# Expert routing spread over projections and batches, pair sums on VectorE, the third layer's bias tables loaded under the sums, and late step sizes on GpSimd

## The chip, the cores and the metric

One core of one Trainium2 chip runs the whole program in one launch. The metric is the device time of that launch in microseconds; lower is better. Five queues of instructions run side by side and meet at semaphores: TensorE (PE), VectorE (DVE), ScalarE (ACT), GpSimd (POOL) and SyncE (SP), which here only issues DMAs.

## What is computed

Four layers on x, 8 sequences of 256 tokens of 128 channels (2048 tokens). Each layer is

```
xn = layernorm(x);  s = mixer(xn);  g = silu(ffn(xn));  x = x + s * g
```

- First layer: a gated linear recurrence, and a dense product of FP8-valued weights.
- Second layer: attention of 16 heads of 8 channels, with binarized weights, and a mixture of 8 experts of which each token takes two. For each choice the reference takes a softmax over the scores that lie within 2 x 0.01 (relative) of the chosen one: `mult = exp(t - s) / sum`, with masked scores left out.
- Third layer: attention of 16 heads with a relative position bias: `scores += 8 * rel_bias[bucket(k - q)]`, 32 buckets, and a gated FFN of 384 units.
- Fourth layer: a selective scan (`h = exp(dt*A)*h + dt*u*B`, `y = sum_n C*h`) with 256 channels and 16 states, and 8 experts of hidden size 512 with a capacity of 256 rows each.

## The kernel before

Everything stays in SBUF with channels on the partitions and the 2048 tokens along the row, in four chunks of 512. Each engine's queue is written out by hand, layer by layer.

**Norm** (`norm_pe`, L222 and L226; `norm_act`, L245 to L257; `norm_dve`, L240): centre by a matmul, square, mean by a matmul, `exp(-0.5 * ln)`, multiply. It follows the chunks of the residual (`residual_dve`, L2103 and L2105).

**Attention** (second and third layer, `attn_pe`, `attn_act`, `attn_dve`, `attn_pool`). First the projections, chunk by chunk: PE projects q and k (L610), ACT writes the upper half in float16 (`high`, L760), DVE the rest (`low`, L841), PE spreads both to strips of 32 rows (L648, L649; six PSUM banks in turn), ACT keeps q (L776) and DVE keeps k (L869). Then the eight sequences ("batches") go through one list of steps that all engines walk, `STEPS[l]`, made from `ORDER`: S1.0 to S1.7 are scores for the row maxima of the next batch (PE L712, DVE L917 or, with the bias, L930), NM negates the maxima (L911), MT puts them beside q (PE L680, L685, ACT L791), S2.0 to S2.7 are the scores again (PE L723, and L731 for the bias) with the exponential by ACT (L804), PV multiplies by v (PE L743), and O, D, R, Y finish the previous batch. Before the first batch all eight S1 steps run alone. S1, S2, MT and two more steps take three pairs of PSUM banks in turn.

**Routing of the second layer** rides on that list through `EXTRA`. TC (`route1_choose`, 13 DVE instructions on 128x128) picks both experts, after S1.7 of the lead-in. TN (`route1_near`, 9 more) makes the masks, in batch 0, followed by CT (counts by PE) and EX (two exponentials by ACT). In batch 1 GpSimd makes the softmax sums (`route1_sums`) and the rows' destinations (`route1_place`, some 50 small instructions in a chain), and from batch 2 it issues 32 indirect DMAs (`route1_dispatch`). XT transposes the tokens. One eighth of the expert weights per batch is split into two float16 halves: ACT writes the upper (WH, L823), GpSimd the lower (`low_weights`, L1262 to L1265, after the routing in each batch), ACT puts the upper back (WB, L826, behind O of the next batch). So WB waits for GpSimd.

**Expert tiles** (`moe_pe`, `moe_act`, `moe_dve`, `moe_pool`): 39 tiles, GpSimd scatters each result to DRAM; `moe_sums` (SP, L1414) reads back the two results of each token, and PE adds each pair by two float32 matmuls with the identity (L1334, 32 products).

**Bias tables of the third layer**: after the second layer's residual the one-hot table is loaded, PE makes the bias rows (L602), ACT scales them (L754), SP writes them to DRAM (L2148) and reads them back as three tables: `bias_q` (3 MB, L2150, into `wf`, which held expert weights) and two halves of `band32` (L2153, into `gate` and `s_sb`). After the projections DVE makes eight small instructions from `bias_q` (L877 to L884), ACT the upper half of `band32` in float16 (L785), GpSimd the lower (L970).

**Scan loop** (`l3_pe`, `l3_act`, `l3_dve`, `l3_pool`, `l3_sync`): 64 tiles of 128x1024. For tile i ACT makes `exp(dt*A)` in PSUM (L1829), GpSimd `dt*u*B` (L2029, four buffers), DVE scans (L1948) and multiplies by C (L1955), PE sums y (L1692); experts ride along at fixed tiles. DVE makes the step sizes of the third and fourth quarter (`step_sizes`, L1925, L1926) after tiles 10 and 12. GpSimd sums the two dispatched halves (L2039) at tiles 14 and 15, PE transposes the sums (L1627) and ACT keeps them (L1800).

## Time and profile before

| | |
|---|---|
| median of 3 runs | 991.57 us (990.63 to 996.0) |
| the profiled execution | 993.26 us, its span 991.5 us |
| PE, DVE busy | 784.5 us (79%), 703.8 us (71%) |
| ACT, POOL busy | 480.4 us, 368.9 us |
| mean granted clock of TensorE | 0.892 |
| chain that ended last | PE 45%, DVE 21%, issue 15%, ACT 11%, POOL 5% |

The stages, in us from the span's start: first layer to 115; second layer's projections 115 to 149, batches to 304, expert tiles to 373, sums, residual and norm to 401; third layer's projections to 433, batches to 612, FFN to 640; fourth layer's preparation to 719, loop to 977, end to 991. No engine is full over the whole, so the shares above say little of one edit; each has to be read from its stage.

### The profile page before, as it was taken

The numbers are of one execution on the slowest core, as the hardware profiler recorded it, in microseconds if no ns is written. First come the engines' busy times: TensorE is split into PE (matmuls) and PEld (weight loads), VectorE is DVE, ScalarE is ACT, GpSimd is POOL, SyncE is SP. The second block draws the span as 40 slices with busy tenths as digits, with TensorE's granted clock in tenths as the row PEclk, the third lists the DMA queues.
The fourth block names the chain that finished last, engine by engine and source line by source line (L and its number), as shares of the span: only waits on it lengthen the run. The fifth ranks groups of instructions, "written<-read, shape, count | busy, mean of one in ns | idle before, by whom it ended". The sixth has DMA issues, their size and how long they took to land.

```text
span 991.5 us, 13685 instructions
## 1 busy us (share of the span) xinstructions
PE 784.5 (79%) x4872; PEld 400.4 (40%) x4872; DVE 703.8 (71%) x1361; ACT 480.4 (48%) x699; POOL 368.9 (37%) x368
## 2 busy tenths in 40 slices
PE   5883795867988996857999998987464678788787
PEld 2331451323435765423555554453121344444344
DVE  2989478656755662586777751268589889889997
ACT  4465352645784443442555563255533245454463
POOL 0000201447662552020000000001797868888860
PEclk9997795777898997885999998978779889999999
DMA  9300000000024113510000000022346525445351
GB/s 364 162 1 0 4 0 1 2 6 29 29 69 134 38 34 91 182 43 1 2 1 2 2 3 1 0 85 69 101 158 189 169 70 205 147 170 177 132 173 43
DMA packets 44339, 76.56 MB, mean 77 GB/s; under 512 B 8479, under 2 KB 30472, under 8 KB 43248
## 3 DMA queue, kind: packets, MB, share of 16 engines
q1 hardware_dynamic: 39952, 67.96, 20.9%
q0 software_dynamic: 4320, 7.72, 2.3%
q8 instruction: 40, 0.66, 0.3%
q14 instruction: 27, 0.22, 0.1%
HBM read 59.83 MB, written 17.01 MB: 78 GB/s over the span
## 4 chain that ended last, share of the span: by engine, by line
PE 45%; DVE 21%; issue 15%; ACT 11%; POOL 5%; DMA 1%; DVEq 0%; SPq 0%; POOLq 0%; ACTq 0%
DVE band L1955 5%; PE ps L743 5%; PE ps L731 4%; DVE arena L1948 4%; PE ps L723 3%; PE ps L290 3%; PE ps L712 2%; ACT arena L804 2%; DVE ttr_out L930 2%; ACT ps L1829 2%; PE ps L610 2%; POOL exp_in L1988 2%; PE ps L704 2%; PE ps L1299 1%; PE ps L649 1%
## 5 line engine op out<-in xcount | busy, mean ns | idle before, releaser
L1948 DVE TENSOR_TENSOR_SCAN arena<-ps,arena 128x1024 f32<-128x1024 f32 x64 | 146.6, 2290 | 27.9 <-ACT ps L1829 13.9
L804 ACT ACTIVATE arena<-ps 128x1024 f32<-128x1024 f32 x128 | 128.3, 1025 | 71.3 <-PE ps L731 54.2
L1829 ACT ACTIVATE ps<-arena,negA 128x1024 f32<-128x1024 f32 x64 | 71.6, 1118 | 131.5 <-DVE arena L1948 131.5
L1692 PE MATMUL ps<-band,w 128*128 128x512 f32 x256 | 123.3, 606 | 0.0
L930 DVE CUSTOM_DVE_ANT_0 ttr_out<-ps,wf 128x256 bf16<-128x256 f32 x256 | 93.1, 420 | 28.3 <-issue 18.0
L1614 PE MATMUL ps<-xq,sel 128*128 128x512 bf16 x128 | 41.2, 405 | 76.7 <-DVE band L1955 67.9
L917 DVE TENSOR_REDUCE arena<-ps 128x4 f32<-128x1024 f32 x64 | 77.1, 1223 | 34.1 <-PE ps L712 33.0
L2029 POOL TENSOR_TENSOR arena<-arena 128x1024 f32<-128x1024 f32 x32 | 76.3, 2387 | 12.5 <-DVE arena L1948 12.1
L712 PE MATMUL ps<-arena 32*128 32x256 f16 x512 | 53.5, 304 | 34.6 <-ACT arena L804 13.3
L1955 DVE TENSOR_TENSOR band<-arena,ps 128x1024 f32<-128x1024 f32 x64 | 76.6, 1197 | 3.5 <-PE ps L1614 3.5
L2029 POOL TENSOR_TENSOR arena<-arena,gate 128x1024 f32<-128x1024 f32 x32 | 75.0, 2361 | 9.9 <-DVE arena L1948 7.7
L1988 POOL DMA_INDIRECT exp_in<-wf,wa x32 | 31.4, 983 | 124.9 <-ACT wf L1729 116.7
L743 PE MATMUL ps<-arena 128*32 128x256 f32 x1024 | 76.2, 420 | 1.0 <-ACT arena L804 0.9
L978 POOL COPY arena<-arena 128x128 f32<-128x128 f32 x32 | 8.5, 296 | 179.5 <-PE ps L743 149.5
L723 PE MATMUL ps<-arena 32*128 32x256 f16 x512 | 62.6, 295 | 9.8 <-DVE arena L917 4.5
L1692 PEld LDWEIGHTS ps<-band,w 128*128 128x128 f32 x256 | 50.4, 197 | 44.6 <-issue 35.7
L731 PE MATMUL ps<-band,ident 128*128 128x192 f16 (+1 forms) x512 | 60.0, 242 | 0.0
L1400 POOL DMA_INDIRECT e_out<-arena,band x39 | 37.9, 972 | 42.8 <-ACT arena L1358 30.6
L1614 PEld LDWEIGHTS ps<-xq,sel 128*128 128x128 bf16 x128 | 8.1, 99 | 108.1 <-DVE band L1955 97.0
L943 POOL MEMSET arena<- 128x512 f16 x2 | 1.0, 524 | 121.6 <-DVE xT L2105 121.6
L791 ACT ACTIVATE arena<-ps 128x1024 f16<-128x1024 f32 x16 | 16.4, 1024 | 54.9 <-PE ps L685 54.9
L712 PEld LDWEIGHTS ps<-arena 32*128 32x128 f16 x512 | 14.7, 95 | 66.0 <-ACT arena L804 19.1
(366 smaller groups left out, 1622.3 us busy)
## 6 DMA issues: line engine op xcount, KB each, us to landing
gate<-b_dram SPq DMA_DIRECT2D x32, 512.0 KB, 4.6
arena<-b_dram SPq DMA_DIRECT2D x32, 512.0 KB, 4.1
wf<-pack1f_dram SPq DMA_DIRECT2D x1, 3076.0 KB, 15.2
wf<-bias_rows SPq DMA_DIRECT2D x1, 3072.0 KB, 10.4
exp_in<-band SPq DMA_DIRECT2D x2, 1032.0 KB, 18.9
exp_out<-band SPq DMA_DIRECT2D x2, 1024.0 KB, 20.8
e_in<-band SPq DMA_DIRECT2D x2, 1024.0 KB, 25.5
arena<-e_out SPq DMA_DIRECT2D x8, 256.0 KB, 4.8
```

The source lines that it names most:

```text
L712: mm = pe.matmul(out_[:, a:a + SEQ], q_st[h, g, (b + 1) * SEQ + qb * P:(b + 1) * SEQ + (qb + 1) * P], k_st[h, g, (b + 1) * SEQ:(b + 2) * S ...
L723: mm = pe.matmul(out_[:, a:a + SEQ], k_st[h, g, b * SEQ + kb * P:b * SEQ + (kb + 1) * P], q_b[par][h, g, :], start=True, stop=(l == 1))
L731: mm = pe.matmul(out_[:, a:a + n], ident16[:, :], band16[:, part, g * HH + 2 * pr + j, 0:n], start=False, stop=(part == 1))
L743: mm = pe.matmul(ps[32 * h:32 * h + 32, 6, (i // 2) * SEQ:(i // 2 + 1) * SEQ], v_b[pp][:, kb, i * HH + h, :], probs[i % 2][:, h, kb, :], s ...
L804: act.activation(probs[g % 2][:, 2 * pr:2 * pr + 2, :, :].rearrange("p h k n -> p (h k n)"), PAIRS[l][("S2", i, b)], ACT.Exp).then_inc(A[" ...
L917: dve.tensor_reduce(row_max[1 - par][:, :, g, 2 * pr:2 * pr + 2].rearrange("p b h -> p h b"), PAIRS[l][("S1", i, b)].rearrange("p (h b n) ...
L930: ins = dve.tensor_tensor_reduce(ttr_out[:, n, :], PAIRS[l][("S1", i, b)][:, n * SEQ:(n + 1) * SEQ], bias_q[:, g * HH + h, WIN - a - SEQ:W ...
L1692: mm = pe.matmul(ps[:, j, :], ident, hc[i % 2][:, j * CH:(j + 1) * CH], start=False, stop=True, skip_group_check=True)
L1829: act.activation(dA_ps, dt3[:, cb, hf * HALF:(hf + 1) * HALF], ACT.Exp, scale=negA[:, cb * STATE + n:cb * STATE + n + 1]).then_inc(M["dA"], 1)
L1948: dve.tensor_tensor_scan(hst[i % 2], dA_ps, dbu[i % 4], 0.0, ALU.mult, ALU.add).then_inc(M["scan"], 1)
L1955: dve.tensor_tensor(hc[i % 2], hst[i % 2], pair(3), ALU.mult).then_inc(M["hc"], 1)
L2029: pool.tensor_tensor(dbu[i % 4], du[:, cb, hf * HALF:(hf + 1) * HALF], b_sb[i % 4], ALU.mult).then_inc(M["dbu"], 1)
```

## The change

**Routing.** The choice is cut into its two rounds (`top1`), which DVE makes behind chunks 0 and 1 of the projections, and the masks behind chunk 2. Both exponentials come before the list of steps, CT in the lead-in before NM, XT one batch earlier, RC at S1.4 of batch 1 and TE at S1.4 of batch 2. On GpSimd the sums run in the lead-in, the totals (`route1_totals`, the first half of the placing) in batch 0, the rest in batch 1; in each batch `low_weights` now comes first. WB stands at S2.4 of the same batch, WH of the next eighth at S2.6.

**Pair sums.** DVE adds the pairs (four instructions of 128x512), PE transposes the sum (16 instructions).

**Bias tables.** The one-hot load, the two products, the scaling and the write to DRAM stand before the sums; the reads stand behind the loads of the sums, the key rows behind them. One half of `band32` goes to `x_rows`, the other still waits for the residual. DVE's eight instructions stand before the projections, ACT's two in them, GpSimd's two during them.

**Step sizes.** Third and fourth quarter on GpSimd: a sum behind tiles 12 and 16, a product behind 14 and 18. DVE's index instructions go from four to two.

The core of the diff:

```diff
-        EXTRA = {(-1, "S1", 7): [("TC", 0)], (0, "S2", 3): [("TN", 0)], (0, "S2", 4): [("CT", 0)], (0, "S2", 5): [("EX", 0), ("EX", 1)],
-                 (2, "S1", 2): [("RC", 0)], (2, "S1", 6): [("TE", 0)],
-                 (1, "S2", 5): [("XT", 0)], (2, "S2", 5): [("XT", 1)]}
+        EXTRA = {(-1, "S1", 7): [("CT", 0)], (0, "S2", 5): [("XT", 0)], (1, "S1", 4): [("RC", 0)], (1, "S2", 5): [("XT", 1)],
+                 (2, "S1", 4): [("TE", 0)]}
...
-                        if (kind, i) == ("O", 0) and b >= 1:
-                            steps.append(("WB", b - 1, b))
-                        if (kind, i) == ("S2", 2) and 0 <= b < BATCH:
-                            steps.append(("WH", b, b))
+                        if (kind, i) == ("S2", 4) and 0 <= b < BATCH:
+                            steps.append(("WB", b, b))
+                        if (kind, i) == ("S2", 6) and 0 <= b < BATCH - 1:
+                            steps.append(("WH", b + 1, b))
...
@@ attn_act @@
+            if l == 2:
+                act.wait_ge(tabs_in, 32)
+                act.wait_ge(S3["zeroed"], 16 * 7)
+                for i, t in enumerate(band32):
+                    act.activation(band16[:, 0, i * HEADS // 2:(i + 1) * HEADS // 2, :], t[:, :, ::-1], ACT.Copy).then_inc(rows_ready, 1)
             high(2)
             high(3)
...
+            if l == 1:
+                route1_exps(act)
+                act.wait_ge(rest_in, 64)
+                act.activation(w_hi, w_part(0), ACT.Copy, scale=W_UP).then_inc(MOE["w_hi"], 1)
...
@@ attn_dve @@
+            step(dve.memset(neg_max, 0.0))
+            if l == 2:
+                dve.wait_ge(rows_out, 32)
+                step(dve.tensor_copy(b_far[:, 0, :], bias_q[:, :, 0]))
...
+                if l == 1:
+                    if c < 2:
+                        route1_choose(dve, c + 1)
+                    elif c == 2:
+                        route1_near(dve)
...
@@ attn_pool @@
                 if l == 1:
+                    if 0 <= b < BATCH:
+                        low_weights(pool, b)
                     if b == -1:
                         route1_both(pool)
+                        route1_sums(pool)
+                    elif b == 0:
+                        route1_totals(pool)
                     elif b == 1:
-                        route1_sums(pool)
                         route1_place(pool)
-                    elif 2 <= b < BATCH:
+                    elif b < BATCH:
                         route1_dispatch(pool, b - 2)
-                    if 0 <= b < BATCH:
-                        low_weights(pool, b)
...
@@ moe_pe @@
+            pe.wait_ge(wa2_in, 16)
+            pe.wait_ge(oh_in, 16)
+            for j in range(2):
+                mm = pe.matmul(ps[0:HEADS, 4 + j, :], WA(1, "rel_bias")[0:BUCKETS, :], onehot_sb[:, j * DIST:(j + 1) * DIST],
+                               start=True, stop=True)
+            mm.then_inc(rows_ps, 1)
             for c in range(NCH):
-                pe.wait_ge(*MOE.at("y_in%d" % c, 32))
+                pe.wait_ge(*MOE.at("y_sum", c + 1))
                 for t in range(4):
-                    for k in range(2):
-                        mm = pe.matmul(ps[:, c, t * P:(t + 1) * P], y1[k][:, 4 * c + t, :], ident, start=(k == 0), stop=(k == 1))
+                    mm = pe.transpose(ps[:, c, t * P:(t + 1) * P], y1[0][:, 4 * c + t, :], ident)
...
@@ moe_dve @@
+            for c in range(NCH):
+                dve.wait_ge(*MOE.at("y_in%d" % c, 32))
+                a_, b_ = (y1[k][:, 4 * c:4 * c + 4, :] for k in range(2))
+                dve.tensor_tensor(a_, a_, b_, ALU.add).then_inc(MOE["y_sum"], 1)
...
@@ l3_dve, l3_pool @@
-                if i in (10, 12):
-                    step_sizes(i // 2 - 3)
...
+                if i in (12, 16):
+                    q = i // 4 - 1
+                    pool.wait_ge(M["plus"], 4 * (q // NB) + 4)
+                    pool.wait_ge(M["ln"], q + 1)
+                    pool.tensor_tensor(quarter(dt3, q), quarter(dt3, q), quarter(sp3, q), ALU.add).then_inc(M["pool_step"], 1)
+                elif i in (14, 18):
+                    q = i // 4 - 1
+                    pool.wait_ge(M["pool_step"], q - 1)
+                    pool.tensor_tensor(quarter(du, q), quarter(dt3, q), quarter(uc, q), ALU.mult).then_inc(M["du"], 1)
```

GpSimd's queue in the second layer, batch 1, before: L978 copies v, L1198 begins the sums, L1211 the placing (its rows up to L1241 are left out), L1262 to L1265 split the weights.

```order
L1265 COPY wf<-w 128x2x256
L978 COPY arena<-arena 128x4x4x8 x2
L1198 TENSOR_TENSOR band<-band 128x128
L1199 COPY band<-band 128x128
...
L1241 TENSOR_SCALAR band<-band 128x8
L1262 TENSOR_SCALAR wf<-wf 128x512
L1263 TENSOR_TENSOR w<-wf,w 128x512
L1265 COPY wf<-w 128x2x256
```

The same place now: L1260 to L1263 split the weights, L1225 begins what is left of the placing.

```order
L966 COPY arena<-arena 128x4x4x8 x2
L1260 TENSOR_SCALAR wf<-wf 128x512
L1261 TENSOR_TENSOR w<-wf,w 128x512
L1263 COPY wf<-w 128x2x256
L1225 TENSOR_TENSOR band<-band 128x8
L1226 TENSOR_SCALAR band<-band 128x8
...
L1239 TENSOR_SCALAR band<-band 128x8
```

The split of the weights moved from behind the chain to right behind the copy of v.

VectorE in the second layer's projections now (L869 keeps k, L843 is `low`, L1037 to L1043 the first round of the choice):

```order
L869 TENSOR_TENSOR arena<-ps,arena 128x512 x4
L843 SCALAR_TENSOR_TENSOR arena<-ps,bq_s,arena 128x512
L843 SCALAR_TENSOR_TENSOR arena<-ps,wa,arena 128x512
L1037 TENSOR_REDUCE band<-band 128x16
L1038 TENSOR_TENSOR band<-band 128x128
L1039 TENSOR_TENSOR band<-band,wc 128x128
L1040 TENSOR_REDUCE band<-band 128x16
L1041 TENSOR_TENSOR band<-band 128x128
L1043 SCALAR_TENSOR_TENSOR band<-band 128x128
L869 TENSOR_TENSOR arena<-ps,arena 128x512 x4
```

Before, the next L869 followed the two `low` at once, and the choice stood behind the eight L917.

SyncE between the expert tiles and the fourth layer's weights, before (`e_out` rows are the sums, `far_keys` the key rows):

```order
L1414 DMA arena<-e_out 128x4x128 x8
L2144 DMA arena<-onehot_dram 32x1024
L2130 DMA arena<-far_keys_dram 5x512 x4
L2148 DMA bias_rows<-arena 16x2x512
L2150 DMA wf<-bias_rows 128x16x384
L2153 DMA gate<-bias_rows 128x8x192
L2153 DMA s_sb<-bias_rows 128x8x192
```

And now:

```order
L2162 DMA bias_rows<-arena 16x2x512
L1423 DMA arena<-e_out 128x4x128 x8
L2165 DMA wf<-bias_rows 128x16x384
L2170 DMA arena<-bias_rows 128x8x192
L2170 DMA s_sb<-bias_rows 128x8x192
L2148 DMA arena<-far_keys_dram 5x512 x4
```

The write of the bias rows moved ahead of the eight loads of the sums, the one-hot load to the start of the expert tiles, and the key rows to the end.

## Rows read from the trace of the kernel before

**Rows 1.** PE in order of time: each batch's L685, and two waits.

```profile
162.82 1.03 PE L685 MATMUL ps<-ident,arena 128*128 128x128 f16 x8 [4.21 <-DVE arena L911]
182.70 1.06 PE L685 MATMUL ps<-ident,arena 128*128 128x128 f16 x8
197.94 0.61 PE L685 MATMUL ps<-ident,arena 128*128 128x128 f16 x8
209.17 0.60 PE L712 MATMUL ps<-arena 32*128 32x256 f16 x4 [7.26 <-ACT arena L804]
222.29 0.62 PE L685 MATMUL ps<-ident,arena 128*128 128x128 f16 x8
231.69 0.60 PE L712 MATMUL ps<-arena 32*128 32x256 f16 x4 [5.42 <-ACT arena L804]
242.91 0.61 PE L685 MATMUL ps<-ident,arena 128*128 128x128 f16 x8
```

**Rows 2.** Batches 4 and 6: stretch, busy PE, PEld, DVE, ACT, POOL, clock, DMA share, GB/s.

```profile
242.90:257.35 14.45, 13.31 (x162) 6.02 (x161) 12.01 (x14) 10.66 (x13) 8.76 (x10) 0.88 0.07 24
271.96:284.80 12.84, 11.68 (x158) 5.38 (x156) 11.71 (x13) 10.66 (x13) 9.41 (x12) 1.00 0.08 27
```

**Rows 3.** ACT's L826 behind GpSimd's split of the weights, batch 2.

```profile
207.58 0.63 ACT L826 ACTIVATE wf<-w 128x512 f16<-128x512 f16 x1 [7.04 <-POOL w L1263]
```

**Rows 4.** DVE in order of time, projections and choice: start, us, what.

```profile
137.41 1.89 DVE L869 TENSOR_TENSOR arena<-ps,arena 128x512 f16<-128x512 f32 x3
148.73 0.06 DVE L873 MEMSET wait_here<- 1x1 f32 x1
158.56 0.28 DVE L1050 TENSOR_REDUCE band<-band 128x16 f32<-128x128 f32 x1
162.33 0.28 DVE L1154 TENSOR_TENSOR band<-band 128x128 f32<-128x128 f32 x1
```

**Rows 5.** The sums: SP, PE, a stretch, last residual, bias rows' products.

```profile
376.17 5.36 SPq L1414 DMA_DIRECT2D arena<-e_out  x8
379.96 10.06 PE L1334 MATMUL ps<-w,arena 128*128 128x128 f32 x64 [7.10 <-DMA arena<-e_out]
380.00:384.00 4.00, 4.00 (x19) 4.00 (x20) 0.00 (x0) 0.22 (x1) 0.00 (x0) 0.50 1.08 298
391.41 0.69 DVE L2105 TENSOR_TENSOR xT<-xT,gate 128x512 f32<-128x512 f32 x1
401.59 2.59 PE L602 MATMUL ps<-arena,wa 32*16 32x512 f32 x4 [3.08 <-DVE xn L240]
```

**Rows 6.** Bias tables: landing of L2150, then ACT, DVE, POOL, PE.

```profile
DMA to landing us min/median/max: 10.4/10.4/10.4
432.45 1.48 ACT L785 ACTIVATE band<-gate 128x1536 f16<-128x1536 f32 x1
434.15 3.01 DVE L884 CAST arena<-b_far 128x16 f16<-128x16 f32 x1
434.00 3.10 POOL L970 TENSOR_TENSOR band<-gate,band 128x1536 f16<-128x1536 f32 x1 [20.42 <-ACT band L785]
441.87 0.61 PE L712 MATMUL ps<-arena 32*128 32x256 f16 x4 [7.90 <-DVE arena L930]
```

**Rows 7.** The loop: DVE's step sizes and a wait, POOL's wait.

```profile
758.70 5.03 DVE L1925 TENSOR_TENSOR arena<-arena 128x1024 f32<-128x1024 f32 x1
765.12 2.29 DVE L1948 TENSOR_TENSOR_SCAN arena<-ps,arena 128x1024 f32<-128x1024 f32 x1
771.98 1.22 DVE L1925 TENSOR_TENSOR arena<-arena 128x1024 f32<-128x1024 f32 x1
775.54 2.29 DVE L1948 TENSOR_TENSOR_SCAN arena<-ps,arena 128x1024 f32<-128x1024 f32 x1
770.79 3.53 POOL L2039 TENSOR_TENSOR wf<-wf,s_sb 128x512 f32<-128x512 f32 x2 [8.16 <-DMA wa<-exp_in]
760.30 2.33 POOL L2029 TENSOR_TENSOR arena<-arena 128x1024 f32<-128x1024 f32 x1
```

More of the change, by code:

```diff
@@ L501, in build @@
         bias_q = wf[:, 0:HEADS * WIN].rearrange("p (h n) -> p h n", h=HEADS)
-        band32 = [t.rearrange("p (h n) -> p h n", n=BAND) for t in (gate[:, 0:HEADS * BAND // 2], s_sb[:, TOK - HEADS * BAND // 2:])]
+        band32 = [t.rearrange("p (h n) -> p h n", n=BAND) for t in (x_rows.rearrange("p t d -> p (t d)")[:, 0:HEADS * BAND // 2], s_sb[:, TOK - HEADS * BAND // 2:])]
         onehot_sb = probs[0].rearrange("p h k n -> p (h k n)")[0:BUCKETS, 0:2 * DIST]
@@ L751, in attn_act @@
             act.wait_ge(*A.at("bq_done", 1))
-            if l == 2:
-                act.wait_ge(rows_ps, 1)
-                act.activation(rows_sb, pair(2)[0:HEADS, :], ACT.Copy, scale=8.0).then_inc(rows_ready, 1)
             def high(n):
@@ L960, in attn_pool @@
             assert made[0] == ALL_ZEROED
+            if l == 2:
+                for i, t in enumerate(band32):
+                    pool.wait_ge(rows_ready, 2 + i)
+                    heads = slice(i * HEADS // 2, (i + 1) * HEADS // 2)
+                    pool.tensor_tensor(band16[:, 1, heads, :], t[:, :, ::-1], band16[:, 0, heads, :], ALU.subtract)\
+                        .then_inc(A["v_zeroed"], 1)
             pool.wait_ge(*A.at("v_done", 4))
@@ L1213, in route1_place @@
                 run = to
+            assert run is runs1[1]
             step(pool.tensor_scalar(tiles1, run[:, NT - 1, :], 1.0 / P, 0.5 - 0.5 / P, ALU.mult, ALU.add))
@@ L1226, in route1_place @@
                 step(ins) if d < 32 else ins.then_inc(MOE["m_in"], 1)
-            step(pool.tensor_tensor(first1, end, tiles1, ALU.subtract))
+        def route1_place(pool):
+            step = route1_step(pool)
+            run, total, before_ = runs1[1], counts_of(1), counts_of(0)
+            step(pool.tensor_tensor(first1, ends_of(3), tiles1, ALU.subtract))
             step(pool.tensor_scalar(first1, first1, float(P), None, ALU.mult))
@@ L1358, in moe_act @@
                     act.activation(e1_sb[n % 4], ps[:, 7, 0:P], ACT.Copy).then_inc(MOE["eo"], 1)
+            act.wait_ge(rows_ps, 1)
+            act.activation(rows_sb, pair(2)[0:HEADS, :], ACT.Copy, scale=8.0).then_inc(rows_ready, 1)
             for c in range(NCH):
```

130 lines of the change are left out of this document (51 added, 79 removed).

## The prediction

> **What bounds the kernel now.** I read the page first, for the two busy shares (PE 79%, DVE 71%) and the chain's 15% "issue", which say that no engine is full and that the time lies in hand-overs. Then the chain of waits in order of time, to find where the chain leaves its usual pattern, and then each engine's timeline at those places. Four places stand out, and the change touches all four.
>
> The second layer's eight batches. PE's L685 marks each batch [rows 1]. Batch 0 takes 182.70 - 162.82 = 19.9 us, batch 1 15.2, batch 2 24.4, batch 3 20.6, and batches 4 and 6 14.45 and 12.84 [rows 2]. In batches 2 and 3 PE sits idle 7.26 and 5.42 us for ACT's exponential [rows 1]. ACT itself is not busy then: its L826 had waited 7.04 us for GpSimd's L1263 [rows 3], which stood in GpSimd's queue behind the chain of small routing instructions (batch 2) and behind six scatters (batch 3). Ahead of batch 0 PE waits 4.21 us for L911 [rows 1]; the choice of experts, 158.56 to 162.61, is what DVE does in that gap [rows 4].
>
> The sums. SP issues the loads at 376.17, PE starts at 379.96 and is busy 10.06 us with 64 half products [rows 5], first at the granted clock of 0.50, which is 1.2 GHz.
>
> The third layer's start. PE spends 2.59 us on the bias rows between norm and projections [rows 5], and after the projections stands still 7.90 us before the second S1 step [rows 6]: DVE is making the small table instructions, of which L884 took 3.01 us for 16 columns, exactly while GpSimd's L970 (3.10 us) ran.
>
> The loop. DVE is its bound: a scan of 2.29 and a product by C follow each other. The step sizes interrupt it from 758.70 to 765.12 and from 771.98 to 775.54 [rows 7].
>
> **The change part by part.** All durations are of the profiled execution, 993.26 us with a span of 991.5; the median is 991.57, so I take the sum of the differences off 991.57.
>
> *Projections of the second layer.* DVE gets 22 instructions on 128x128 (6, then 7, then 9). Thirteen of them took 162.61 - 158.56 = 4.05 us, 0.31 each with their step waits [rows 4], so 22 cost 6.9 us. What room has DVE? From 137.41 to 148.73 it makes twelve L869 of 0.63 (7.6 us) and two `low`, for which I allow 1.5: some 2.3 us are free. PE can run six banks ahead, which shifts this room but adds none. So the projections end 6.9 - 2.3 = 4.6 us later; the bounds are 2 (more room) and 9 (all 6.9, and PE, waiting more, falls to 1.2 GHz).
>
> *Lead-in.* The choice goes: -4.05 us. What is late next is MT's first product, which now follows CT in the ring of three pairs and waits for the last reduction; it was done early. I take +0.8, one L685 or less (0.61 to 1.03).
>
> *Batch 0* loses CT and the nine mask instructions on DVE, whose product delayed S1; it gains one transposition with its 1.02 us eviction by ACT. The stretch ran at 1.2 GHz before and starts so again. I take -2.6, between +1 and -6 (a free batch). Batch 1 swaps one XT for the other: 0.
>
> *Batches 2 and 3.* GpSimd's split comes first in each batch, so L826's wait goes. GpSimd then has per batch 0.5 for v, 3.3 for the split and at most 6 scatters of 1.3: under 12 us, inside a batch. The split is ready some 5.5 us into the batch, S2.4 comes at about 8. Both batches come to a free one, between 12.84 and 14.45 [rows 2]; I take 13.7: -10.7 and -6.9. Batches 4 and 5 may lose the dip of the clock (0.88 against 1.00 in batch 6), since WB and WH no longer stand ahead of the early exponentials: -0.7 and -0.9, and -0.5 at the tail. For PE leaving the upper level more often than I think I give back 1. Sum for the second layer: 4.6 - 4.05 + 0.8 - 2.6 - 10.7 - 6.9 - 1.6 - 0.5 + 1 = -20.0, bounds -10 and -27. Behind it the last scatters end some 4 us later relative to the batches; before, the first load of expert rows landed 5 us ahead of its use, so this costs nothing, or up to 2 if that room is smaller.
>
> *Sums.* The bias products (2.59), ACT's scaling and one DMA issue now stand before the loads: these start at 377.1 instead of 376.17, +0.9. The data is in by about 385.5 (at 298 GB/s the DMAs were done at 384.6 [rows 5]). DVE adds the last pair by 386.2, PE transposes in 0.6, ACT's last gate is at 387.5 against 390.7, but DVE makes its four residual pairs (1.4 us each) only after its four sums, so the last is at 391.9 against 392.1 [rows 5]. The norm starts 1.8 earlier on ACT and is paced by PE: -1.2, between -3 and +3.
>
> Before, PE had come back to 2.4 GHz inside the 64 products. The 16 transposes are a quarter of the records, and the norm's products could run at 1.2 GHz, 1.7 us instead of 0.9 for a pair; that is the +3. The Trainium skill (TensorE: Matmul & The Clock Gate, "PE-mode transpose") says that transposes don't count as busy for the clock in the way products do. No row here shows a transpose alone raising or not raising the clock; by the page the term would be about +2 instead of -1.2.
>
> *Bias rows out of the norm's shadow:* -2.59 for L602, of which I give back 0.4 for a colder start of the projections: -2.2.
>
> *Tables.* `bias_q` is queued right behind the sums' loads; with its 10.4 us to landing [rows 6] it is there at about 396, the second `band32`, behind the residual, at about 403. DVE asks at 400, ACT at 411: hidden, with 4 us to spare; beyond that each us late is lost. ACT's two L785 (2 x 1.48) now stand between the eviction of the output weights and `high` of chunk 1, with PE, and DVE's `low`, behind them. Six banks cover part: +1.6, between 0 and 3. The lead-in then starts without the tables: of the 7.90 us, S1's usual 1.03 and its first step remain: -6.3 (-5.5 to -7).
>
> GpSimd's two L970 now run beside DVE's L869. Before, L884, which reads and writes SBUF alone, was held up by L970. The L869 and `low` have one operand in PSUM, as the scan and L1955 have, which kept 2.29 and 1.20 us beside GpSimd's L2029. So I charge nothing.
>
> *Loop.* Two interruptions go: 6.42 + 3.56 = -10.0. GpSimd gets four instructions of 2.33 each [rows 7] and two small ones. The first two fall into its wait of 8.16 us [rows 7], covered. The last two, behind tiles 16 and 18, aren't: GpSimd, three tiles ahead before, is about level at tiles 16 to 19, which I price at 1.5; two index instructions less on DVE give 0.5: -9.0, between -4 and -10.5.
>
> Sum: -20.0 - 1.2 - 2.2 + 1.6 - 6.3 - 9.0 = -37.1. **991.57 - 37.1 = 954.5 us.**
>
> **The rivals.**
>
> *A, the forecast:* 954.5, own range 948 to 961. Chance 0.60.
>
> *B, the batches keep half.* PE drops to 1.2 GHz in the busier projections and in batch 0 and the batches settle at 14.5 or above with WB waiting now and then: the second layer gives 10, not 20: 964.5. For it: batches 4 and 5 stood at 0.88 without any GpSimd wait. Against it: batch 6 ran at 1.00 with the same work [rows 2]. Chance 0.18.
>
> *C, GpSimd's products cost DVE what they save.* L1925 took 5.03 us with GpSimd's L2029 beside it and 1.22 without [rows 7]: two engines, one in the other's way. If scans were held by the four new instructions, 4 x 2.33 = 9.3 come back: 963.8. Against it: scans ran at 2.29 beside L2029 throughout. The Trainium skill (Perfetto Trace Analysis, "Optimizing Scalar/DVE Operations") warns that work moved between these two might not help because they share an SBUF port. Chance 0.12.
>
> *D, the tables are late.* If the 3 MB land at 405 or later, DVE's first `low` and all behind it wait, 8 us: 962.5. For it: the same queue carries the sums' 2 MB first. Against it: 298 GB/s on those. Chance 0.05.
>
> *E, slower: low clock through the batches.* If the more even mix kept PE at 1.2 GHz from the projections on, a batch's 13.3 us of PE at 0.88 [rows 2] become 23.4; over seven batches +68 against my 13.7, hence 1022. It makes the kernel slower only once the mean batch is over 13.7 + 37/7 = 19 us, as batch 0 was. Against it: batches 1 and 6. Chance 0.02; another 0.03 is for a sum of small losses that leaves no change.
>
> **How the numbers follow.** A, B, C and D (0.95) are all faster by over 0.5% (below 986.6), which is also about what a measurement of this kernel tells from no change; 0.03 within, 0.02 slower. The range takes A with its bounds, and B, C and D up to a little above their centres: 946 to 967.
>
> **What would show it.** In the profile after: the choice's instructions between the L869, and the first S1 step 4 to 5 us later; no wait of ACT's L826 for GpSimd over 1 us; eight batches of 12.8 to 14.5 us but the first two; the four DVE additions at about 381 to 386, and the norm ending 1 us earlier; no pause over 2 us before the second S1 step of the third layer; scans every 3.5 us from tile 0 to 14, and the scan of tile 15 about 9 us earlier relative to tile 0. I am wrong if the second layer's batches still hold a GpSimd wait, if DVE's first `low` in the third layer waits for a DMA, or if scans wait for L2029 in many tiles.

## The result and the profile after

The changed kernel takes 968.27 us (median of 4 runs, 967.06 to 969.62) against 992.83 us of the kernel before in the same runs (990.63 to 996.0): ratio 0.9751, 95% interval 0.9719 to 0.9783. It is faster, as forecast, but by 24.6 us and not 37. 968.3 is nearer to rival B's time (964.5) than to the forecast's, and lies 1.3 us above the range. Of the 13.8 us between forecast and result, 1.3 is the kernel before itself: the forecast took its 37.1 off a median of 991.57, which is 992.83 with a fourth run. The profiled span is 967.5 us against 991.5.

The working is checked most easily by milestones that both traces have. Each row is the length of a piece (us, before and after), and what the prediction said of it.

| Piece | before | after | measured | predicted |
|---|---|---|---|---|
| second layer's projections (scaling of bq to first S1 maximum) | 34.47 | 37.49 | +3.0 | +4.6 |
| lead-in to the first MT | 13.32 | 10.02 | -3.3 | -3.25 |
| batch 0 | 19.88 | 17.15 | -2.7 | -2.6 |
| batch 1 | 15.24 | 16.82 | +1.6 | 0 |
| batches 2 and 3 | 44.97 | 31.27 | -13.7 | -17.6 |
| batches 4, 5 and 6 | 41.70 | 46.09 | +4.4 | -1.6 |
| batch 7 and tail | 18.96 | 19.67 | +0.7 | -0.5 (+1 given back) |
| experts, sums and norm, to its end | 98.02 | 98.28 | +0.3 | -1.2 |
| bias rows' products | 2.52 | 0 | -2.5 | -2.2 |
| third layer's projections | 29.25 | 30.67 | +1.4 | +1.6 |
| its lead-in (S1) | 20.27 | 13.72 | -6.5 | -6.3 |
| its first batch | 21.86 | 24.07 | +2.2 | 0 |
| loop, first scan to last | 253.76 | 244.70 | -9.1 | -9.0 |

The changed trace comes to this point 0.6 us later, and the pieces not listed differ by -0.4 together; the sum is -24.0.

The second layer is where the time is missing: 20 us were promised and 10.0 came (the first seven rows). Its batches by stretches (length, busy time of PE, PEld, DVE, ACT and POOL, granted clock, DMA share, GB/s), to be read beside [rows 2]:

```profile
180.27:197.09 16.82, 13.67 (x168) 6.80 (x167) 13.14 (x15) 11.50 (x14) 9.78 (x25) 0.90 0.00 1
197.09:213.08 15.99, 13.05 (x159) 5.89 (x158) 13.89 (x17) 10.62 (x13) 10.64 (x13) 0.89 0.07 22
213.08:228.36 15.28, 12.96 (x159) 5.85 (x158) 12.85 (x14) 10.66 (x13) 8.70 (x10) 0.89 0.09 29
228.36:244.57 16.21, 13.94 (x160) 6.20 (x159) 12.94 (x14) 10.59 (x13) 8.70 (x10) 0.79 0.07 22
244.57:260.36 15.79, 12.90 (x159) 5.76 (x158) 13.03 (x14) 10.59 (x13) 10.21 (x13) 0.89 0.08 27
260.36:274.45 14.09, 11.39 (x155) 5.16 (x154) 12.74 (x13) 10.59 (x13) 10.29 (x12) 1.00 0.08 25
```

No batch is at the 13.7 us of the forecast, though no instruction stands at a semaphore for GpSimd: the waits of [rows 1] and [rows 3] are gone. What TensorE waits for between 163 and 294 us says more (what waits, for whom: us in all, times, longest):

```profile
PE ps L690 <- DVE arena L892: 10.0, 8, 1.7
PE ps L715 <- DVE arena L905: 5.1, 9, 1.1
PE ps L715 <- ACT arena L798: 3.6, 8, 0.5
```

L892 ends VectorE's chain of three instructions (reciprocal of the denominators, its upper half as f16, the rest). VectorE in batch 4 of the changed kernel, and GpSimd at that time:

```profile
231.80 0.95 DVE L888 RECIPROCAL arena<-ps 128x128 f32<-128x128 f32 x1
232.78 0.92 DVE L890 CAST arena<-arena 128x128 f16<-128x128 f32 x1
233.73 0.70 DVE L892 TENSOR_TENSOR arena<-arena 128x128 f16<-128x128 f32 x1
```

```profile
230.88 1.49 POOL L1260 TENSOR_SCALAR wf<-wf 128x512 f32<-128x512 f32 x1
232.46 1.16 POOL L1261 TENSOR_TENSOR w<-wf,w 128x512 f16<-128x512 f32 x1
233.68 0.61 POOL L1263 COPY wf<-w 128x512 f16<-128x512 f16 x1
```

The two instructions that read and write SBUF take 0.92 and 0.70. In batch 6 of the kernel before, where GpSimd issued scatters at that time, they took 0.23 and 0.29:

```profile
276.22 0.23 DVE L902 CAST arena<-arena 128x128 f16<-128x128 f32 x1
276.48 0.29 DVE L904 TENSOR_TENSOR arena<-arena 128x128 f16<-128x128 f32 x1
```

The reciprocal reads PSUM and takes 0.95 in both. TensorE starts R late and runs the PV product behind it at 1.2 GHz, 1.94 us, where others take 1.07.

```profile
234.49 0.29 PE L690 MATMUL ps<-arena,spread 128*128 128x128 f16 x1 [1.23 <-DVE arena L892]
236.00 1.94 PE L735 MATMUL ps<-arena 128*32 128x256 f32 x16
```

The loop came out at the number forecast, but not by its working. The first row below is the scan of tile 15, the second that of tile 16, the third one of VectorE's two index instructions, the last GpSimd's work on the expert rows:

```profile
761.33 2.29 DVE L1959 TENSOR_TENSOR_SCAN arena<-ps,arena 128x1024 f32<-128x1024 f32 x1 [3.34 <-POOL arena L2036]
766.09 2.29 DVE L1959 TENSOR_TENSOR_SCAN arena<-ps,arena 128x1024 f32<-128x1024 f32 x1 [1.36 <-POOL arena L2036]
770.70 2.28 DVE L1983 SCALAR_TENSOR_TENSOR wa<-wa 128x32 uint32<-128x32 f32 x1
756.45 2.49 POOL L2057 TENSOR_TENSOR wf<-wf,s_sb 128x512 f32<-128x512 f32 x2 [3.82 <-DMA wa<-exp_in]
```

Scans now wait for GpSimd, which in turn waits for rows of the experts from DRAM, as in [rows 7]. The index instruction of 32 columns takes 2.28 beside a product of GpSimd's; in step_sizes_on_dve, below, the same one takes 0.19.

### The profile page after: what moved, and what is told of

The parts are those of the page before. It is cut to its first block, busy times and chain, and to the rows that moved or that the text cites. A ratio compares the mean times of both kernels' runs of the same rounds, so it can differ in the third digit from the quotient of the medians.

```text
span 967.5 us, 13578 instructions
## 1 busy us (share of the span) xinstructions
PE 774.8 (80%) x4811; PEld 393.7 (41%) x4824; DVE 695.5 (72%) x1357; ACT 479.2 (50%) x699; POOL 375.8 (39%) x374
## 4 chain that ended last, share of the span: by engine, by line
PE 47%; DVE 21%; issue 13%; ACT 11%; POOL 4%; DMA 2%; SPq 2%; DVEq 0%; POOLq 0%
PE ps L735 6%; PE ps L723 5%; DVE band L1966 4%; DVE arena L1959 3%; PE ps L715 3%; PE ps L704 3%; PE ps L290 3%; POOL arena L2036 2%; POOL exp_in L1995 2%; DVE ttr_out L918 2%; PE ps L696 2%; DVE arena L905 2%; ACT ps L1838 2%; PE ps L1314 2%; PE ps L1297 2%
## 5 line engine op out<-in xcount | busy, mean ns | idle before, releaser
L918 DVE CUSTOM_DVE_ANT_0 ttr_out<-ps,wf 128x256 bf16<-128x256 f32 x256 | 93.1, 420 | 30.7 <-issue 21.7
L1623 PE MATMUL ps<-xq,sel 128*128 128x512 bf16 x116 | 37.5, 398 | 71.9 <-DVE band L1966 62.6
L704 PE MATMUL ps<-arena 32*128 32x256 f16 x512 | 54.2, 305 | 13.7 <-DVE arena L918 6.6
L723 PEld LDWEIGHTS ps<-band,ident 128*128 128x128 f16 x512 | 33.9, 100 | 19.3 <-issue 8.3
L715 PEld LDWEIGHTS ps<-arena 32*128 32x128 f16 x512 | 21.4, 95 | 49.0 <-issue 17.7
## 6 DMA issues: line engine op xcount, KB each, us to landing
wf<-pack1f_dram SPq DMA_DIRECT2D x1, 3076.0 KB, 15.5
wf<-bias_rows SPq DMA_DIRECT2D x1, 3072.0 KB, 12.8
exp_out<-band SPq DMA_DIRECT2D x2, 1024.0 KB, 21.2
```

The source lines that it names most:

```text
L704: mm = pe.matmul(out_[:, a:a + SEQ], q_st[h, g, (b + 1) * SEQ + qb * P:(b + 1) * SEQ + (qb + 1) * P], k_st[h, g, (b + 1) * SEQ:(b + 2) * S ...
L715: mm = pe.matmul(out_[:, a:a + SEQ], k_st[h, g, b * SEQ + kb * P:b * SEQ + (kb + 1) * P], q_b[par][h, g, :], start=True, stop=(l == 1))
L723: mm = pe.matmul(out_[:, a:a + n], ident16[:, :], band16[:, part, g * HH + 2 * pr + j, 0:n], start=False, stop=(part == 1))
L918: ins = dve.tensor_tensor_reduce(ttr_out[:, n, :], PAIRS[l][("S1", i, b)][:, n * SEQ:(n + 1) * SEQ], bias_q[:, g * HH + h, WIN - a - SEQ:W ...
```

## The experiments

Theory P: GpSimd's split beside VectorE's chain holds the chain up, and this is why the batches stay at 16 us. Theory A: ScalarE's new order does it. Theory C: TensorE's clock does it by itself. For the loop: the interruptions were the 9 us, or something else was. Ratios are to the kernel before; the changed kernel has 0.9751 (0.9719 to 0.9783). Each time is a median of four executions, of which one was profiled; every stretch and wait comes from that one.

**split_waits**

```diff
+                    if 1 <= b < BATCH:
+                        pool.wait_ge(*A.at("d_done", b))
                     if 0 <= b < BATCH:
                         low_weights(pool, b)
```

> The changed kernel, but GpSimd's split of batches 1 to 7 waits until VectorE's three reciprocal instructions of that batch (D chain) are through. Theory P (GpSimd's split beside VectorE's chain): in the changed kernel the chain takes 0.95 + 0.92 + 0.70 = 2.6 us, without the split beside it 1.5 (as in batch 6 of the kernel before), and the PV step behind it runs at the upper clock more often (1.07 instead of 1.94); so 1.1 to 2 us off each of batches 1 to 6: the second layer's batches 7 to 12 us shorter, 956 to 961 us in all. Theory A (ScalarE's new order, with WB and WH among the exponentials, sets the batch's length): unchanged, 967 to 969. Theory C (the clock comes first, and falls whatever GpSimd does): chain shorter, but the batches shorter by under 3 us, 965 to 968.

958.58 us, ratio 0.9624 (0.9588 to 0.9659): 9.7 us less than the changed kernel, for one more wait. TensorE's waits for L892 fall from 10.0 to 2.6, and batches 2 to 6 from 77.4 to 69.8:

```profile
PE ps L690 <- DVE arena L892: 2.6, 3, 1.7
PE ps L1290 <- DMA gate<-e_in: 1.2, 1, 1.2
```

```profile
197.93:212.08 14.15, 12.74 (x159) 5.63 (x158) 13.18 (x17) 10.59 (x13) 7.62 (x10) 0.88 0.03 11
226.48:241.32 14.84, 12.90 (x159) 5.86 (x158) 12.21 (x14) 10.59 (x13) 9.13 (x11) 0.89 0.07 24
241.32:254.65 13.33, 11.72 (x160) 5.26 (x158) 11.75 (x14) 10.59 (x13) 7.08 (x10) 1.00 0.05 17
```

P holds and A falls, since ScalarE's order is the same. C explains the rest: a batch is at 13.1 to 13.3 with the clock at 1.00 and at 14.2 to 14.8 with 0.88. Not all of the 9.7 lies there. The experts start 5.2 us earlier (288.95 against 294.12), though 1.2 are lost to their first load, which is late now (the second row). The third layer is shorter by 2.7 up to its first MT and by 2.0 in its first batch, with no edit there: TensorE left 1.2 GHz earlier. Those 4.7 are no gain to count on, since both stretches differ by as much between other profiles of the same code (28.0 to 30.7 us for the projections, 21.0 to 24.1 for the first batch).

The batches themselves repeat. The seven other kernels whose split still runs beside the chain (choice_in_one_piece, the two sums runs and the first four of the loop, all below) have casts of 0.91 to 0.99 there and take 77.4 to 78.8 us for batches 2 to 6. The three in which it doesn't (split_waits, split_old_place, split_rows_steps) have casts of 0.23 to 0.29 and take 69.4 to 69.8.

**split_mixed**

```diff
+                    if b == 1:
+                        pool.wait_ge(*A.at("d_done", b))
+                    elif 2 <= b < BATCH:
+                        route1_dispatch(pool, b - 2, 0)
                     if 0 <= b < BATCH:
                         low_weights(pool, b)
```

Here `route1_dispatch` with 0 issues the first two scatters and with 1, at its old place, the others.

> The changed kernel, but GpSimd issues two of its scatters ahead of the split in batches 2 to 7, and waits for the chain only in batch 1. Theory P: as split_waits or up to 2 us better, since GpSimd doesn't stand idle and the next batch's copy of v isn't late: 955 to 961. Theory A: 967 to 969. Theory C: 965 to 968. If issuing indirect DMAs is what slows the chain (against P), the casts take over 0.4 us here.

966.14 us, 0.9688 (0.9635 to 0.9742), above P's range, and an interval that overlaps the changed kernel's. But it shows how finely this depends on time, as two scatters don't quite reach over the chain. In batch 5 the first scatter came late, behind two small instructions, and lay over the whole chain. In batch 6 the cast began 0.6 us before the end of the second scatter and was held until the split had begun:

```profile
247.58 0.23 DVE L890 CAST arena<-arena 128x128 f16<-128x128 f32 x1
263.42 0.67 DVE L890 CAST arena<-arena 128x128 f16<-128x128 f32 x1
264.12 0.70 DVE L892 TENSOR_TENSOR arena<-arena 128x128 f16<-128x128 f32 x1
```

```profile
263.04 0.98 POOL L1259 DMA_INDIRECT e_in<-arena,band  x1 [0.30 <-issue]
264.03 1.53 POOL L1265 TENSOR_SCALAR wf<-wf 128x512 f32<-128x512 f32 x1
```

Computing on SBUF costs the chain its 0.7 to 1 us. Issuing a scatter mostly costs it nothing: 0.23 in batches 4 to 7 of the kernel before and in batches 2 to 7 of split_old_place, each beside a scatter. It isn't always free, though. In batches 3, 4 and 6 here the cast began before the split did, and by its usual 0.23 it would have ended before it too; in batch 7 it took 0.45 in the changed kernel and 0.33 here beside scatters alone. As spans on GpSimd are rough, where the hold begins stays open. Batches 3, 4 and 6, with casts of 0.67, take 15.9, 15.5 and 15.35, and batch 2, with 0.23, 14.5. Batch 5 has 0.23 too and takes 15.8: there ScalarE's WB waits 0.82 us for the split, which now comes later. The clock differs too (0.79 in batch 3, 0.88 or 0.89 in the others), so that these lengths don't show the price of the cast by itself.

**split_old_place**

```diff
-                        if (kind, i) == ("S2", 4) and 0 <= b < BATCH:
-                            steps.append(("WB", b, b))
-                        if (kind, i) == ("S2", 6) and 0 <= b < BATCH - 1:
-                            steps.append(("WH", b + 1, b))
+                        if (kind, i) == ("O", 0) and b >= 1:
+                            steps.append(("WB", b - 1, b))
+                        if (kind, i) == ("S2", 2) and 1 <= b < BATCH:
+                            steps.append(("WH", b, b))
```

and `low_weights` behind the routing work on GpSimd.

> The changed kernel with the split where the kernel before had it: GpSimd behind the routing work and the scatters, ScalarE's copy back behind the next batch's O, its copy out behind S2.2; all else as changed. Theory P: batches 4 to 6 go back to 14.5, 14.6 and 12.8 (now 16.2, 15.8, 14.3: -4.4), batches 2 and 3 wait again for GpSimd, though less than before since sums and totals come earlier: batch 3 keeps its 5 us wait; net -4 to +3, 964 to 971. Theory A: the same direction, as ScalarE's order goes back too. It tells what the new place was worth by itself: the prediction said 19 us for batches 2 to 6; then this would be 985.

961.33 us, 0.9644 (0.9600 to 0.9687): better than the changed kernel by 7, outside what I expected. Its batches are 17.4, 17.2, 14.25, 14.6, 13.1, 14.6 and 12.8: the waits of [rows 1] don't come back. So the earlier routing work is enough to remove them, without the new place of the split; whether that place alone would have done it, no run shows. In batch 2 it was the chain of small instructions in front of the split. Batch 3 is another case: its six scatters still stand in front of the split here. Before, GpSimd had first stood still for 9.28 us until ScalarE had the transposed tokens, and this wait is gone with the earlier XT:

```profile
217.96 0.28 POOL L1253 TENSOR_SCALAR arena<-band 128x16 f32<-128x16 f32 x1 [9.28 <-ACT arena L816]
```

The casts are back at 0.23 to 0.28, with ScalarE's order and GpSimd's both as before; it is split_waits that tells the two apart. The new place of the split by itself costs about 7 us.

**choice_in_one_piece** puts the 22 choice instructions as one piece behind the projections.

> The changed kernel with the 22 instructions of the choice of experts not between the projections but in one piece behind them, ahead of the first S1 steps. Prediction (22 cost 6.9 us, 2.3 of them hidden beside the projections): first row maximum 2.3 us later than in the changed kernel: 155.4 instead of 153.1, and 970 in all. Rival H (beside the projections they are hidden nearly in full, since VectorE waits there for TensorE): 5 to 7 us later, 974. Rival N (nothing is hidden): the same time, 968.

970.51 us, 0.9777 (0.9747 to 0.9808). From the scaling of bq to the first S1 maximum it takes 41.48 us against 37.49 changed and 34.47 before. The piece takes 6.8 us (148.63 to 155.44), as priced, of which 4.0 are hidden among the projections where I had put 2.3. Of the whole, 2.2 us show, and the intervals overlap.

**sums_on_pe** and **sums_interleaved**

```diff
...
-                    mm = pe.transpose(ps[:, c, t * P:(t + 1) * P], y1[0][:, 4 * c + t, :], ident)
+                    for k in range(2):
+                        mm = pe.matmul(ps[:, c, t * P:(t + 1) * P], y1[k][:, 4 * c + t, :], ident, start=(k == 0), stop=(k == 1))
...
```

The first also takes VectorE's four additions out, and TensorE waits for the loads instead. The second leaves only the last chunk's residual behind the sums:

```diff
                 dve.tensor_tensor(a_, a_, b_, ALU.add).then_inc(MOE["y_sum"], 1)
+                if c:
+                    moe_residual(dve, (c - 1,))
```

> The changed kernel with the pair sums on TensorE again, by two products with the identity for each tile as in the kernel before; all else as changed. It prices the part by itself. The prediction: 1.2 us slower than the changed kernel. Rival T (16 transposes leave TensorE at 1.2 GHz and four norm products take 3.8 instead of 1.9 us, as the profile after shows, which eats the gain): 0 plus or minus 1.5 us, with the first four norm products at 1.9 us here. Rival, clock wins: 1 to 3 us faster.

> The changed kernel, but VectorE makes the residual of chunk c-1 right behind the pair sum of chunk c, instead of all four behind the four sums. Theory S (the norm starts late because VectorE does its residuals last): first norm product at 376.5 instead of 379.3, the norm over 1.5 to 2.5 us earlier, 966 in all. Rival (TensorE at 1.2 GHz and ScalarE's table load pace the norm): under 1 us, nothing measurable.

967.61 us, 0.9750 (0.9728 to 0.9771), and 969.71 us, 0.9778 (0.9749 to 0.9807): nothing that the intervals can tell, either way. The norm's first four products, in the changed kernel and in sums_on_pe:

```profile
379.26 3.78 PE L222 MATMUL ps<-xT,centre 128*128 128x512 f32 x4 [0.21 <-DVE xT L2123]
```

```profile
381.54 1.88 PE L222 MATMUL ps<-xT,centre 128*128 128x512 f32 x4
```

Behind the transposes TensorE is still at 1.2 GHz and behind the 64 products it isn't; the 1.9 us lost eat most of the 2.3 by which the norm starts earlier. The Trainium skill (TensorE: Matmul & The Clock Gate, "PE-mode transpose") says that transposes don't count as busy in the way products do. The 3.78 against 1.88 fit it and don't show it, since another difference would do as well: the 16 transposes come in four bursts of 1.12 us with waits for VectorE between, 4.5 us busy out of 7.7, and the 64 products keep TensorE busy for 10 us on end. Interleaving could not start the norm early, since TensorE makes all transposes first in its queue, and the last of them waits for VectorE's last sum.

**step_sizes_on_dve**, **step_sizes_late**, **expert_rows_later**, **rows_and_steps_later**: the loop. The first puts both step sizes back on VectorE behind tiles 10 and 12. The others:

```diff
-                if i in (12, 16):
...
-                elif i in (14, 18):
...
+                if i in (28, 42):
...
+                elif i in (30, 45):
...
```

```diff
-        XE_SLOT, UP_SLOT, UP_STEP, MIX_SLOT = 12, 16, 4, 54
+        XE_SLOT, UP_SLOT, UP_STEP, MIX_SLOT = 13, 17, 4, 54
```

(14 and 18 in rows_and_steps_later, which has the late step sizes too), with the loads of the rows issued at the old point.

> The changed kernel with the last two step sizes back on VectorE (behind tiles 10 and 12 of the loop), index instructions as changed. Loop theory (VectorE's two interruptions of 6.4 and 3.6 us were the 9.0 us that the loop lost): +8.5 to +9.5, 977 us, span from first scan to last 253 instead of 244.7. Rival (the gain came from the order of DMAs or the fewer index instructions): under +3, 968 to 971.

> The changed kernel, but GpSimd makes the third and fourth step size behind tiles 28/30 and 42/45 of the loop instead of 12/14 and 16/18 (they are needed from tiles 32 and 48 on). Theory L (in the changed kernel GpSimd's own four products make scans wait for it in tiles 15 to 21, which gives back 6 of the 9.5 us that VectorE saved): loop from first to last scan 239 to 241 us instead of 244.7, so 4 to 6 us less than the changed kernel, 962 to 965. Rival (scans of tiles 15 to 21 are held by the expert rows that arrive there, whatever GpSimd does besides): 244, unchanged. Second rival (the products now hold the scans at 28 to 32 and 42 to 48 instead): 244 to 247.

> The changed kernel, but the loop's expert work starts one tile later (XE_SLOT 13 and UP_SLOT 17 instead of 12 and 16), while SP issues the loads of the expert rows where it did; the step sizes stay on GpSimd behind tiles 12 to 18. Theory R (GpSimd waits for the expert rows, which land 52 us after the first scan in every run so far, and dbu of tile 15 stands behind that wait): scan 15 comes at 53.7 instead of 56.9 after the first. Theory G (GpSimd then has more to do than the scans leave it: ten dbu of 2.36, four step size products of 2.35, 5 us for the rows): part of it comes back by tile 21; loop 241 to 244 instead of 244.7. If R is false: 244.7.

> The changed kernel with the expert work two tiles later (XE_SLOT 14, UP_SLOT 18, loads issued where they were) and the step sizes behind tiles 28/30 and 42/45. Theory R and G together: no scan between 11 and 21 waits over 1 us for GpSimd: loop 237.5 to 240 instead of 244.7, so 5 to 7 us off the whole: 961 to 963. Rival (the last expert then ends too late for the mixing at tile 54, and the scans wait there): the gain at 21 is there, and up to 5 us are lost behind tile 50. Rival 2 (no effect, R false): 244.

| Scan of tile, us after the first | 10 | 13 | 15 | 17 | 21 | 63 | median us, ratio (interval) |
|---|---|---|---|---|---|---|---|
| before | 36.10 | 56.26 | 66.70 | 76.25 | 94.87 | 253.76 | |
| changed | 36.03 | 46.63 | 56.90 | 68.47 | 85.80 | 244.70 | 968.27, 0.9751 (0.9719 to 0.9783) |
| step_sizes_on_dve | 36.03 | 56.41 | 64.31 | 72.37 | 88.81 | 247.73 | 973.12, 0.9789 (0.9756 to 0.9822) |
| step_sizes_late | 36.18 | 46.78 | 56.85 | 67.29 | 85.02 | 244.31 | 969.16, 0.9787 (0.9748 to 0.9827) |
| expert_rows_later | 36.15 | 46.76 | 53.82 | 64.11 | 83.61 | 245.92 | 969.95, 0.9773 (0.9741 to 0.9805) |
| rows_and_steps_later | 36.88 | 47.48 | 54.55 | 62.44 | 81.95 | 243.37 | 966.58, 0.9731 (0.9687 to 0.9775) |

The interruptions are worth 9.8 us at tile 13, as forecast, but 6.8 are given back by tile 21, so that moving the step sizes is worth 3.0 (247.73 - 244.70) in the loop and 4.9 in the median. That lies between the loop theory (8.5 to 9.5) and its rival (under 3). The scan of tile 15 waits 3.34 us for GpSimd where in step_sizes_on_dve it waits 0.95 for ScalarE, tile 16's waits 1.36, the index instruction is held for 2.1, and a product by C waits 0.84 for TensorE: 6.7 of the 6.8. The main reason is in GpSimd's queue: its work on the expert rows stands behind tile 14's product and waits for their load, and none of these edits moves the load. SyncE issues its four parts behind the row of tile 15, which waits for GpSimd's product of tile 11: the first 36.9 us after the first scan and the last at 44.9 to 45.8, in every profile. In the profiles the work starts 51.5 (before), 52.0 (changed), 51.7 and 52.0 us after the first scan, whether VectorE was interrupted or not. Before, VectorE had not come further by then. Theory L, that GpSimd's own products are to blame, falls with step_sizes_late. One tile later, scan 15 is at 53.82:

```profile
753.64 2.49 POOL L2057 TENSOR_TENSOR wf<-wf,s_sb 128x512 f32<-128x512 f32 x2 [1.63 <-DMA wa<-exp_in]
765.60 2.29 DVE L1959 TENSOR_TENSOR_SCAN arena<-ps,arena 128x1024 f32<-128x1024 f32 x1 [2.52 <-POOL arena L2036]
778.03 2.29 DVE L1959 TENSOR_TENSOR_SCAN arena<-ps,arena 128x1024 f32<-128x1024 f32 x1 [4.27 <-ACT ps L1838]
```

That wait is gone, and others stand in its place: tile 19's scan 4.27 us for ScalarE, which stands before the eviction of the last expert rows until TensorE has transposed them, and in tile 58 of rows_and_steps_later another 3.26 for TensorE at the mixing, as its first rival had it. R holds at tile 15, where the scan was to come at 53.7. Its gain is lost again by the end: the loop takes 245.92 and 243.37, against 241 to 244 and 237.5 to 240 expected.

The remaining 6.0 us of the loop (253.76 - 247.73) came with no edit of the loop but the index instructions. Before, TensorE fell to 1.2 GHz there (0.51 from 780 to 785 us, and again 0.50 from 800 to 805), at the same places of step_sizes_on_dve it did not; the first place, clock behind the busy columns:

```profile
775.00:790.00 15.00, 8.82 (x23) 4.48 (x24) 11.16 (x9) 4.44 (x5) 14.13 (x8) 0.77 0.44 146
```

```profile
759.50:774.50 15.00, 9.26 (x33) 4.27 (x31) 13.70 (x10) 4.51 (x6) 14.85 (x8) 1.00 0.43 144
```

Of the 6.0, 1.5 are the index instructions (2.70 before, 1.21 here). The other 4.5 are two waits (4.7 together). The scan of tile 15 waits 3.50 for ScalarE before and 0.95 here: ScalarE's exponential stands behind the eviction of the expert rows, this behind TensorE's transposes, and these behind TensorE's sums for y, which take 3.62 us before and 1.88 here. And the product by C of tile 19 waits 2.13 for TensorE before, and not here:

```profile
779.83 3.62 PE L1692 MATMUL ps<-band,w 128*128 128x512 f32 x4
785.98 2.29 DVE L1948 TENSOR_TENSOR_SCAN arena<-ps,arena 128x1024 f32<-128x1024 f32 x1 [3.50 <-ACT ps L1829]
808.14 1.22 DVE L1955 TENSOR_TENSOR band<-arena,ps 128x1024 f32<-128x1024 f32 x1 [2.13 <-PE ps L1614]
```

```profile
764.07 1.88 PE L1701 MATMUL ps<-band,w 128*128 128x512 f32 x4
```

So the 4.5 are the price of TensorE at 1.2 GHz at these two tiles. Why it was there in the one profile and not in the other was not tested.

**three_mended** and **split_rows_steps**: the sums of parts.

> Three things at once: three scatters ahead of GpSimd's split in batches 2 to 7 and a wait for VectorE's chain in batch 1 (so that the split never runs beside the chain), the late step sizes, and the residuals between the sums. If the three are independent: 968 minus 10 (batches) minus 5 (loop) minus 2 (sums): 951, between 948 and 955. If batch lengths are set by the clock and not by the chain: 958 to 962. In the batches the cast is to take 0.23 and the difference 0.29 in all of them.

970.67 us, 0.9779 (0.9757 to 0.9801): a miss by 20 us. With three scatters ahead, casts take 0.23 in batches 1 to 6, but batches 2 and 5 take 17.4 and 18.4 us. There `route1_dispatch` first makes two small instructions, and 0.8 to 0.9 us pass from the second to the first scatter. The split now stands behind all this and begins 5.7 to 5.8 us after the copy of v, against 4.3 in batches 3 and 6, with ScalarE's WB and the exponentials behind it:

```profile
209.54 0.63 ACT L813 ACTIVATE wf<-w 128x512 f16<-128x512 f16 x1 [1.62 <-POOL w L1266]
255.93 0.63 ACT L813 ACTIVATE wf<-w 128x512 f16<-128x512 f16 x1 [2.12 <-POOL w L1266]
```

It is the wait of [rows 3] again, made by moving two things past each other. The rest of the 3 to 4 us by which these two batches are longer goes with the clock, 0.80 there and 0.88 or 0.89 in batches 3 and 4.

> Three things together: GpSimd's split waits for VectorE's chain (as in split_waits, -9.7 us there), expert work one tile later, step sizes behind tiles 28/30 and 42/45. If batches and loop are independent: 968 - 9.7 - 4 to -6 = 952 to 955. If what the loop gains is held by the arrival of the rows in another way: 958.

956.96 us, 0.9641 (0.9580 to 0.9701), above the 952 to 955 of independent parts, with single runs from 950.88 to 962.53. It beats the changed kernel; against split_waits its ratio tells no difference, though its loop is 241.5 us where that has 244.4. Its batches 0 to 6 are 15.8, 14.25, 14.2, 14.3, 14.8, 13.3 and 13.1, and the second layer as a whole (from the scaling of bq to the experts' first product) takes 169.76 us, against 188.54 before, 178.51 changed and 174.39 in split_waits: 18.8 of the 20 us promised. Its batches have the same code as split_waits; of the 4.6 between the two, 4.1 are batches 0 and 1, which take 17.3 and 16.9 there at a clock of 0.62 and 0.80, and 15.8 and 14.25 here at 0.71 and 1.00. The experts now wait 2.64 us for their first rows: the scatters are next to bound.

## Why the prediction was wrong

- **The free batch (batches 1 to 6), wrong, and 11.5 of the 13 us.** The step "Both batches come to a free one ... I take 13.7" took the batch length from [rows 2], where GpSimd issued scatters beside VectorE's chain, and used it for an order in which GpSimd computes there. Measured for batches 2 to 6: 15.99, 15.28, 16.21, 15.79 and 14.09, together 9.9 us more than forecast, of which split_waits gets 7.6 back. The other 1.6 are batch 1, and the split is not their cause: that batch takes 16.87 in split_waits too, with a cast of 0.23, and 14.25 in split_rows_steps at a clock of 1.00. What decides the clock there stays open. The split beside the chain took some 5 to 6 us at the experts' start and 7 to 10 of the whole (split_old_place, split_waits), part of it by way of the clock. I had the evidence: [rows 6] has a VectorE instruction of 16 columns at 3.01 us beside GpSimd's L970, and the prediction says of it that L884 "reads and writes SBUF alone". I asked that question of the tables and the loop, and not of the batches. Rival B had the size, 964.5, with another cause; rival C had the cause, but in the loop.
- **Waits of batches 2 and 3, half right.** They are gone, but split_old_place is without them too, with the split in its old place: the earlier routing and the earlier XT are enough. For batch 3 the prediction named the six scatters, which still stand there; it was the 9.28 us that GpSimd waited in front of them.
- **Choice and lead-in, right but for one size:** 6.8 us for the piece (6.9) and -3.3 for the lead-in (-3.25). The choice cost +3.0 and not +4.6, since about 4.0 us of it are hidden beside the projections and not 2.3.
- **Sums: -1.2 was +0.3.** The bound "+3" named what happened, TensorE at 1.2 GHz in the norm (3.78 us for four products, 1.88 in sums_on_pe). I should have given that more weight than an early start of VectorE. Whether the transposes or the waits between them kept the clock low is not shown.
- **Bias rows and tables, right:** -2.5, +1.4 and -6.5 against -2.2, +1.6 and -6.3. The +1.4 compares two profiles whose first products both ran at 1.2 GHz (3.78 and 3.75 us); where they ran at 2.4, the projections took 28.0 and not 30.7. VectorE's L869 kept its 0.63 beside GpSimd's two products of 3.11, so that charging nothing for them was right. The tables were not late (rival D):

```profile
392.40 3.75 PE L602 MATMUL ps<-xn,wa 128*128 128x512 f32 x4 [3.07 <-DVE wa L822]
392.99 0.17 DVE L829 COPY b_far<-wf 128x16 f32<-128x16 f32 x1
```

- **The third layer's first batch, a term that the prediction doesn't have:** +2.2 in this profile. TensorE stays at 1.2 GHz longer:

```profile
443.00:450.00 7.00, 7.00 (x51) 2.98 (x50) 2.92 (x18) 3.07 (x3) 0.00 (x0) 0.50 0.01 4
450.00:460.86 10.86, 10.70 (x99) 4.99 (x98) 5.01 (x30) 4.09 (x4) 0.00 (x0) 0.73 0.00 0
```

Before, the last 8.49 us of that batch had 0.97. It is no price of the edit: with the same third layer and the same lead-in, the profiles have 21.0, 21.2, 21.4, 22.1 and 24.1 for this batch, on both sides of the 21.86 before. What decides between them stays open.
- **The loop, right by luck: two errors met.** -9.0 was to be 10.0 less 1.5 given back plus 0.5. Measured: 9.8 less 6.8, plus 1.5 for the index instructions and 4.5 in which TensorE kept its clock. I took GpSimd's wait of 8.16 [rows 7] for cover, and it was a load that comes no earlier when VectorE does: the next bound. Rival C's cause, VectorE held by GpSimd, has 2.1 of the 6.8.

## What to carry to other kernels

When an instruction of GpSimd moves, ask what VectorE does in that microsecond: one that has both ends in SBUF may stand still while GpSimd computes, one that reads PSUM did not in any run, and a scatter being issued seldom held anybody. Before you take an engine's wait as room, ask what ends it: a load whose issue the edit doesn't move lands when it did before, and becomes the bound for whoever gets faster. And check a sum piece by piece even when it comes out right: here two errors of 5 us met in the loop.

## What the runs showed of the hardware

- A cast of 128x128 with both ends in SBUF takes 0.23 us, and up to 0.98 beside GpSimd's split of the weights (instructions of 0.6 to 1.5 us). Beside GpSimd's small routing instructions (0.2 to 0.5 us) it took 0.23 to 0.28, and the subtraction behind it 0.29 to 0.58; a small instruction of 32 columns takes 0.19 and 2.28 (L1983, beside a GpSimd product of 2.35); 128x1024 takes 1.22 and 5.13. A reciprocal that reads PSUM takes 0.95 either way, a scan 2.29. The Trainium skill (SBUF — State Buffer, "SBUF: two separate sides") says that VectorE and GpSimd share one pair of ports, held for a whole instruction, when VectorE has two SBUF inputs or runs in a mode with two ports; the trace agrees for these: waits to the end of the GpSimd instruction in progress, for 128x1024 over two products, and none where an operand is in PSUM.
- Beside an indirect DMA being issued on GpSimd these casts mostly took their 0.23 (batches 4 to 7 before, batches 2 to 7 in split_old_place), but 0.33 to 0.46 in batch 7 of four profiles, and 0.67 in split_mixed where the split followed.
- Four norm products took 3.78 us behind 16 transposes with waits between them (granted clock 0.50, 1.2 GHz) and 1.88 behind 64 products without (1.00, 2.4 GHz).
- The same code gave 15.8 and 17.3 us for the second layer's batch 0 in different profiles, by when TensorE left 1.2 GHz. Differences of 2 to 3 us in a stretch of one profile tell nothing by themselves.
